# A graph network on one core: clears in the key phase, DVE's order in two projections, an output phase without loops, and aggregation's end sums on two queues

## What is computed

```python
h = jnp.maximum(_layernorm(x, axis=-1), 0.0)
x = x + _L0_gnn_ref(h, edge_index, ...)      # three attention convolutions, one head, sigmoid
h = jnp.maximum(_layernorm(x, axis=-1), 0.0)
x = x + _L1_gnn_ref(h, deg_isqrt[:, None], src, dst, edge_type_100, ...)   # relational, 4 bases
h = jnp.maximum(_layernorm(x, axis=-1), 0.0)
x = x + _L2_gnn_ref(h, edge_index, ...)      # attention, 8 heads
h = jnp.maximum(_layernorm(x, axis=-1), 0.0)
x = x + _L3_gnn_ref(h, edge_index, ...)      # messages from both ends of an edge, mean, linear
```

## Time and profile before

| | |
|---|---|
| three runs | 3926.29, 3939.06, 3943.65 us, median 3939.06 |
| profiled execution | 3923.35 us, its span 3921.4 us |
| busy share of the span | PE 58%, DVE 58%, POOL 55%, ACT 41% |
| mean granted TensorE clock | 0.79 |
| DMA, mean | 97 GB/s |

### The profile page before, as it was taken

How to read it: one execution, slowest core, us unless ns; L and a number is a source line. 1 busy time by engine, 2 the same in 40 slices (tenths; PEclk the granted TensorE clock), 3 DMA queues, 4 the chain that set the end, 5 groups by cost and what they waited for, 6 DMA issues and landing times. The chain is left out here.

```text
span 3921.4 us, 53964 instructions
## 1 busy us (share of the span) xinstructions
PE 2263.7 (58%) x12833; PEld 1777.4 (45%) x12833; DVE 2282.0 (58%) x8009; ACT 1610.7 (41%) x3565; POOL 2157.8 (55%) x2121
## 2 busy tenths in 40 slices
PE   1035899999898565465565567754526443344333
PEld 1023676676677554364464444434425332233222
DVE  4154999999898785334345378866575333333233
ACT  0005999999997573223323322324411222122100
POOL 3618765575564332581185255546500588888755
PEclk9998999999999786577577588887756666666665
DMA  2140122332231454651663733333304333333253
GB/s 64 27 181 20 44 90 87 100 103 87 87 92 39 133 157 116 161 139 42 186 174 87 203 95 99 87 98 81 90 16 118 109 74 64 75 74 65 51 145 117
DMA packets 569029, 380.48 MB, mean 97 GB/s; under 512 B 51389, under 2 KB 511942, under 8 KB 568386
## 3 DMA queue, kind: packets, MB, share of 16 engines
q1 hardware_dynamic: 510050, 329.99, 28.7%
q0 software_dynamic: 56000, 46.29, 6.4%
q10 hardware_dynamic: 2720, 1.23, 0.2%
HBM read 249.08 MB, written 153.32 MB: 103 GB/s over the span
## 5 line engine op out<-in xcount | busy, mean ns | idle before, releaser
L1309 POOL DMA_INDIRECT p_a<-t_d,k_map_ix x300 | 309.1, 1030 | 291.3 <-DMA p_a<-t_d 241.1
L807 POOL TENSOR_TENSOR a_rs<-a_ve,w_neg_half 128x16 f32<-128x16 f32 x113 | 330.1, 2922 | 241.7 <-DVE a_ve L743 227.7
L833 ACT ACTIVATE a_nr<-a_xb,a_nm,a_rs 128x128 f32<-128x128 f32 x882 | 369.9, 487 | 26.1 <-POOL a_nm L809 26.1
L2064 POOL DMA_INDIRECT e_a<-t_d,e_ix x200 | 210.4, 1052 | 277.1 <-DMA e_a<-t_s 219.2
L895 PE MATMUL a_ps<-w_ident,a_nr 128*128 128x128 f32 x1568 | 245.6, 280 | 128.8 <-DVE a_xb L754 47.3
L903 PE MATMUL a_ps<-a_ht,w_aug 128*128 128x512 f32 x588 | 312.7, 616 | 2.4 <-DVE a_ht L710 2.4
L895 PEld LDWEIGHTS a_ps<-w_ident,a_nr 128*128 128x128 f32 x1568 | 179.9, 143 | 277.0 <-issue 244.5
L1431 PE MATMUL p_pm<-w_aug,p_ht 128*128 128x130 f32 (+1 forms) x1600 | 277.1, 343 | 7.6 <-ACT p_ht L1392 3.8
L710 DVE TENSOR_TENSOR a_ht<-a_ps,a_ht 128x512 f32<-128x512 f32 x294 | 201.5, 686 | 134.7 <-ACT a_ps L848 111.0
L1431 PEld LDWEIGHTS p_pm<-w_aug,p_ht 128*128 128x128 f32 x1600 | 261.4, 250 | 21.4 <-ACT p_ht L1392 11.9
L1789 PE MATMUL c_pq<-layer_src,c_sel 128*128 (+1 forms) x800 | 194.3, 420 | 124.7 <-ACT c_sel L1760 72.2
(11 more groups left out here) (358 smaller groups left out, 6449.0 us busy)
## 6 DMA issues: line engine op xcount, KB each, us to landing
t_s<-p_a SPq DMA_DIRECT2D x100, 256.0 KB
c_a<-t_d SPq DMA_DIRECT2D x100, 256.0 KB
t_d<-c_a SPq DMA_DIRECT2D x100, 256.0 KB
a_xa<-in_x SPq DMA_DIRECT2D x98, 256.0 KB
out<-a_xb SPq DMA_DIRECT2D x98, 256.0 KB, 2.0
p_a<-t_s SPq DMA_DIRECT2D x75, 256.0 KB
p_a<-t_d SPq DMA_DIRECT2D x75, 256.0 KB
t_acc<-q_zt SPq DMA_DIRECT2D x3, 2171.5 KB
```

The lines of the kernel that those rows point to most:

```text
L807: nc.gpsimd.tensor_tensor(RS[:, z, :], VE[:, z, :], w["neg_half"][:, None, 0:J].to_broadcast([P, LNS, J]), ALU.pow).then_inc(s_rstd.sem, 1)
L833: last = nc.scalar.activation(NR[k][:, T.at(NORM[k], 2), cols(j)], normed_rows(T, k)[:, cols(j)], ACT.Identity, bias=NM[:, T.at(1, SHORT), ...
L1309: eng.indirect_dma_start(out=A[:, g, SRC, j, :], out_offset=None, in_=t[f"d{r}"], in_offset=bass.IndirectOffsetOnAxis(ap=k["map_ix"][:, b ...
L2064: eng.indirect_dma_start(out=A[:, g, side, j, :], out_offset=None, in_=t[f"d{r}"], in_offset=bass.IndirectOffsetOnAxis(ap=IX[:, g, what, j ...
```

## The change

- `keys`: behind each of the 100 scatters POOL clears a tile `idle` of 128x256, waiting for the clear before.
- `project`: in rounds 0 and 4 DVE's step n is now residual and hold first, statistics after. In round 0: residual(n-4), hold(n-3), turn(n). In round 4 the residual follows its hold by no step: hold(n-3), residual(n-3), turn(n). Rounds 1 and 2 keep their order.
- `aggregate`: SP issues four of the eight end-sum transfers, ahead of its loads and behind the last bank copy; ACT issues the other four. The two source-row transfers go ahead of ACT's last bank copy, with a semaphore of their own. ACT's sigmoid stands two blocks behind the widening, not one.
- `edge_outputs`: unrolled, a ring of 8 instead of 5, indices read in place instead of copied, a clear behind each scatter; TensorE and DVE take turn(n) and sum of block n ahead of product and end of block n-1.

```diff
@@ -219,6 +219,7 @@
         TMQ = sb("tmq", [P, T])
         DUMPC = sb("dumpc", [P, 1], I32)
         M1 = sb("m1", [P, T], I32)
+        IDLE, s_idle = sb("idle", [P, 256]), sem("idle")
         OF = sb("of", [T, 2, P])
         ENDROW = sb("endrow", [T, 2, T])
         OTHER = sb("other", [T, 2, T])
@@ -302,6 +303,9 @@
             for c in range(T):
                 eng.indirect_dma_start(out=t["maps"], out_offset=bass.IndirectOffsetOnAxis(ap=M1[:, c:c + 1], axis=0),
                                        in_=ID[:, c:c + 1], in_offset=None, bounds_check=NODES * WORDS - 1, oob_is_err=False).then_inc(s_map1, 16)
+                if c:
+                    eng.wait_ge(s_idle, c)
+                nc.gpsimd.memset(IDLE[:, :], 0.0).then_inc(s_idle, 1)
             eng.wait_ge(s_map1, 16 * T)
 
         @block.tensor
@@ -1358,16 +1362,19 @@
                 there(eng, b, SRC)
                 v.tensor_tensor(A[:, g, SRC, :, :], A[:, g, SRC, :, :], grow, ALU.add).then_inc(s_next, 1)
 
-            holds, residuals = (3, 4) if norm else (0, 1)
+            holds = 3 if norm else 0
+            residuals = holds if normed else holds + 1
             for n in range(BLOCKS + residuals):
+                if not normed and 0 <= n - residuals:
+                    residual(n - residuals)
+                if 0 <= n - holds < BLOCKS:
+                    hold(n - holds)
+                if normed and 0 <= n - residuals:
+                    residual(n - residuals)
                 if norm and n <= BLOCKS:
                     if n < BLOCKS:
                         there(eng, n)
                     mo.turn(eng, lambda m: A[:, n % RING, m // J, m % J, :], n, BLOCKS - 1)
-                if 0 <= n - residuals:
-                    residual(n - residuals)
-                if 0 <= n - holds < BLOCKS:
-                    hold(n - holds)
 
         @block.scalar
         def _(eng):
@@ -1634,6 +1641,14 @@
         ON_ACT = 13 if H == 1 else 0
         in_bank = lambda n: range(n * J, min(n * J + J, BLOCKS))
 
+        s_rows_in = sem("rows_in")
+
+        def end_sums(eng, tiles):
+
+            for j in tiles:
+                for s in range(2):
+                    eng.dma_start(ENDT[j:T:J, s, :], PART[2 * j + s:2 * j + s + 1, 0:BLOCKS, :]).then_inc(s_endt, 16)
+
         @block.sync
         def _(eng):
             def load(b, g):
@@ -1662,6 +1677,8 @@
                 carry_waits(eng, w)
                 eng.dma_start(block_rows(t[f"d{r + 1}"], b), A[:, g, :, :]).then_inc(s_out[g], 16)
 
+            eng.wait_ge(s_part, BANKS)
+            end_sums(eng, range(J // 2))
             stream(eng, (load, 0), *([(store_sel, 2)] if first else []), (store, 3))
             for g in range(GE):
                 eng.wait_ge(s_out[g], 16 * ROUNDS_E)
@@ -1709,7 +1726,7 @@
             for b in range(ON_ACT, BLOCKS):
                 v.tensor_tensor(heads_of(rows("dst", b)), heads_of(rows("dst", b)), over(tiles_of(ws, b)[:, :, 0:H]), ALU.mult).then_inc(s_own, 1)
             eng.wait_ge(s_new_pe, 1)
-            eng.wait_ge(s_endt, 16 * (2 * J + 2))
+            eng.wait_ge(s_rows_in, 32)
             v.tensor_tensor(NEW[:, :, :], PN[0:T, :, :], ENDT[:, 2:4, :], ALU.add).then_inc(s_new, 1)
             if ON_ACT:
                 eng.wait_ge(s_own_act, ON_ACT)
@@ -1738,15 +1755,14 @@
                             m = b * J + j
                             last = nc.scalar.activation(keep["dst"][:, m, 0:C], keep["dst"][:, m, 0:C], ACT.Copy, scale=ws[:, m, 0:1])
                         last.then_inc(s_own_act, 1)
+                if n == BANKS - 1:
+                    eng.wait_ge(s_ms, BLOCKS)
+                    for s, row in enumerate((0, P - 1)):
+                        eng.dma_start(ENDT[:, 2 + s:3 + s, :], keep["src"][row:row + 1, :, 0:C]).then_inc(s_rows_in, 16)
                 eng.wait_ge(s_part_pe, n + 1)
                 nc.scalar.activation(PART[:, n * J:n * J + len(in_bank(n)), :], PQ[n][0:2 * J, 0:len(in_bank(n)), :], ACT.Copy).then_inc(s_part, 1)
             eng.wait_ge(s_part, BANKS)
-            for j in range(J):
-                for s in range(2):
-                    eng.dma_start(ENDT[j:T:J, s, :], PART[2 * j + s:2 * j + s + 1, 0:BLOCKS, :]).then_inc(s_endt, 16)
-            eng.wait_ge(s_ms, BLOCKS)
-            for n, row in enumerate((0, P - 1)):
-                eng.dma_start(ENDT[:, 2 + n:3 + n, :], keep["src"][row:row + 1, :, 0:C]).then_inc(s_endt, 16)
+            end_sums(eng, range(J // 2, J))
             eng.wait_ge(s_new, 1)
             for n, row in enumerate((0, P - 1)):
                 eng.dma_start(keep["src"][row:row + 1, :, 0:C], NEW[:, n:n + 1, :]).then_inc(s_fix, 16)
@@ -1763,7 +1779,7 @@
                 wait(eng, s_u, b + 1)
                 nc.scalar.activation(PS[g][:, :, :], PS[g][:, :, :], ACT.Sigmoid).then_inc(s_sig, 1)
 
-            stream(eng, (widen, 0), *([(squash, 1)] if sigmoid else []))
+            stream(eng, (widen, 0), *([(squash, 2)] if sigmoid else []))
 
         @block.tensor
         def _(eng):
@@ -1775,7 +1791,7 @@
                         last = nc.tensor.matmul(PQ[n][0:2 * J, b - n * J, :], k["end_of"][:, m, :], keep["src"][:, m, 0:C],
                                                 start=j == 0, stop=j == J - 1)
                 last.then_inc(s_part_pe, 1)
-            eng.wait_ge(s_endt, 16 * (2 * J + 2))
+            eng.wait_ge(s_endt, 16 * 2 * J)
             for n in range(2):
                 for s in range(2):
                     last = nc.tensor.matmul(PN[0:T, n, :], k["cross"][:, 2 * n + s, :], ENDT[:, s, :], start=s == 0, stop=s == 1)
@@ edge_outputs
+    RING, BANKS = 8, 2
...
-        IX = sb("ix", [P, GE, J], I32)
-        ACC = sb("acc", [P, GE, J, M])
...
+        ACC = sb("acc", [P, RING, J, M])
...
+        IDLE = sb("idle", [P, 256])
...
         @block.gpsimd
         def _(eng):
...
+            for b in range(BLOCKS):
+                g = b % RING
+                eng.wait_ge(s_out_in, b + 1)
                 for j in range(J):
+                    m = b * J + j
-                    eng.indirect_dma_start(out=out, out_offset=bass.IndirectOffsetOnAxis(ap=IX[:, g, j:j + 1], axis=0),
+                    eng.indirect_dma_start(out=out, out_offset=bass.IndirectOffsetOnAxis(ap=k["out_s_ix"][:, m:m + 1], axis=0),
...
+                    if m:
+                        eng.wait_ge(s_idle, m)
+                    nc.gpsimd.memset(IDLE[:, :], 0.0).then_inc(s_idle, 1)
...
         @block.vector
...
-            stream(eng, (count_, 0), (finish, 1), (summed, 0))
+            for n in range(BLOCKS + 1):
+                if n < BLOCKS:
+                    summed(n)
+                if n:
+                    finish(n - 1)
...
         @block.tensor
...
-            stream(eng, (turn, 0), (product, 0))
+            for n in range(BLOCKS + 1):
+                if n < BLOCKS:
+                    turn(n)
+                if n:
+                    product(n - 1)
```

More of the change, by code:

```diff
@@ L2251, in edge_outputs @@
+        s_cnt, s_tp, s_s, s_mm, s_up, s_out_in, s_idle = (sem(n) for n in "cnt tp s mm up out_in idle".split())
+        s_load, s_out = ([sem(f"{n}{g}") for g in range(RING)] for n in ("load", "out"))
         block = ctx.enter_context(nc.Block())
-        before = lambda b, g: b - (1 if g == 0 else 2)
+        uses = lambda b: b // RING + 1
         @block.sync
         def _(eng):
-            def load(b, g):
-                wait(eng, s_out[g], (b // GE) * (16 * J))
-                carry_waits(eng, w)
+            for b in range(BLOCKS):
+                g = b % RING
+                if b >= RING:
+                    eng.wait_ge(s_out[g], (uses(b) - 1) * (16 * J))
```

75 lines of the change are left out of this document (35 added, 40 removed).

## The result

The changed kernel took 4086.39 us (median of four runs, 4079.69 to 4090.51) and the kernel before, beside it, 3940.16: a ratio of 1.038 (95% interval 1.035 to 1.041), 146 us slower. Its profiled execution took 4085.83 us, +162.5 against that of before, with a mean granted clock of 0.78.

A forecast was written before the change was run, and what follows sets the result against it. No engine bounds the kernel: each stage's longest loop sets its length, and stages add up. Terms -61 + 132 + 97 - 12 + 5 - 4 = +157 gave 4080 us profiled, 4096 us as median; range 4020 to 4145 us.

The forecast's parts named there:

- DVE order, round 0: `project`, round 0: hold ahead of statistics makes the path serial, 11.2 us a block against 5.46, +132 us (+95 to +144).
- if ACT's copy could pass apply: `project`: a condition under which the second rival had the earlier residual only free the ring; ACT's code order spoke against it.
- the second rival: `project`: the new order pays, round 0 unchanged and round 4 -53 us, giving 3814 us, faster; chance 0.07.
- Round 4: `project`, round 4: the serial path, now with the residual in it, replaces 8.30 us a block, +97 us (+51 to +106).
- I take 12.5: `project`, round 4: us a block assumed, between 10.5 with the fast product and 12.7 with the slow one.
- Key phase: `keys`: clears between scatters let TensorE's signals through, next stage loads at 210 instead of 271.08, -61 us (-66 to -50).
- 3 us for last landings and the barrier: Key phase: time allowed from the end of POOL's last scatter, at 207, to the next stage's load at 210.
- its weak bound of -50: Key phase: the gain if the table's zeroing and the scatters disturb each other, -50 us.
- Aggregate: `aggregate`, four rounds: split end sums and earlier row transfers -12 us (-16 to 0), later sigmoid +5 (0 to +8).
- the loads stay covered: `aggregate`: SP's loads, queued behind the end sums, are needed only over 10 us after the last bank copy.
- edge_outputs: `edge_outputs`: without loops, with a ring of 8 and clears, POOL alone sets the pace, 149 us, -4 us (-8 to +3).
- the third rival: Key phase: clears do not free TensorE's signal, waits stay and POOL takes 20 us longer, 4200 us; chance 0.07.
- the fourth: `project`: the reordering moves nothing that a wait rests on, 3867 us; chance 0.02.

The follow-up runs named there:

- e1_stats_first: The changed kernel with DVE's order of the kernel before in `project` (statistics, then residual, then hold): 3877.13 us, ratio 1.007 to the kernel before.
- e2_act_copies_first: The changed kernel, but ACT takes the copy of block n-1 and the sigmoid of n-2 ahead of apply(n) in rounds 0 and 4: 4075.45 us.
- e3_act_pe_first: As e2_act_copies_first, and TensorE also takes product(n-1) ahead of turn(n) in rounds 0 and 4: 3813.06 us, ratio 0.990.
- e6_before_clears: The kernel before with clears behind the key phase's scatters and nothing else of the change: 3889.67 us, ratio 0.986.
- e7_lag_one: The kernel of e3_act_pe_first with the sigmoid one block behind the widening again: 3824.25 us, ratio 0.969.
- e4_residual_early: The changed kernel with statistics first again in rounds 0 and 4, round 4's residual following its hold: 3830.60 us, ratio 0.995.

## Why the prediction was right, and where not

The sum was +157 us, the profiles show +162.5, the medians +146. The mechanisms came as written. That the touched stages add up to +156 is in part luck: the terms were off by 4, 13, 9, 5 and 2 us, in both directions.

**DVE order, round 0: +132 predicted, +128 found.** The steps are in the rows: shift to the destination's hold 7.66 us (7.26 read), hold to the next shift 3.67 (3.66 read), distances of 11.1 on average in the steady part (11.2 taken). That both holds wait for TensorE (though DVE waits longer for ACT's squashed rows ahead of them), that ACT and TensorE stand idle behind the shift, and that the clock falls came as written. `e1_stats_first` shows that all of it is DVE's order. One sentence was short of the truth: "if ACT's copy could pass apply" is not the point on which the second rival turns, as `e2_act_copies_first` shows; TensorE's product has to pass its transposes too. `e3_act_pe_first` also moved the squash ahead of apply, with the copy.

**Round 4: +97 predicted, +84 found.** The step that failed is "I take 12.5". One distance was 12.5, but it alternates with 11.4, the product taking 3.81 or 2.71 us: 23 x (12.5 - 11.95) is the 13 us. I had taken the slow end for most blocks, when the two ends, 10.5 and 12.7, stood in the text. (The upper bound does not follow from the text either: 12.7 us a block gives 23 x 4.4 = +101, not +106.)
The Trainium skill (TensorE: Matmul & The Clock Gate, section "HAM oscillation — how this bites in real kernels") says that a TensorE which waits between bursts starts each at half clock. The trace agrees: the transposes that open the blocks at 2852.3 and 2864.8 have a granted clock of 0.50. The step from there to whole blocks at the slow end, +106 here and +144 in round 0, was the prediction's own, and the measured terms are 22 and 16 us below it. Within most bursts the clock went back to 1.00: the product of 3.81 us had a mean granted clock of 0.54 and the next, of 2.71 us, 0.78, where the one of 4.05 us in the kernel before had 0.50.

**Key phase: -61 predicted, -52 found.** That the clears let TensorE's signals through was right, and POOL's end came at 209 instead of 207. (With free landings the stated sum gives 207 - 271 = -64, not -66.) The step that failed is "3 us for last landings and the barrier": it was 10.4, of which 8.2 are POOL's DRAIN. The term landed near its weak bound of -50, but not for the reason given there: zeroing and scatters do not disturb each other. The Trainium skill's rule (SBUF — State Buffer, section "SBUF: two separate sides"), by which only VectorE and GpSimd hold each other up and TensorE waits on nobody, speaks of access to SBUF. Read as if it covered signals too, it gave a loss of 20 us here; `e6_before_clears` shows a gain of 53.8.

**Aggregate: -12 and +5 predicted, -1.8 together found.** On the averages over fourteen profiles given above it is -11.4 for the end sums and +6.7 for the later sigmoid, -4.7 together: both terms were near, and the pair of profiles shows less because the kernel before was at its fastest in rounds 1 and 4. But -11.4 hides two errors. The cross product came 5 us earlier, not 3.3: with two queues the last transfer is issued 3.3 us after the bank copy as taken, but TensorE goes on 1.6 us behind it and not 3.1, as the two row transfers are no longer among those that it waits for. And "the loads stay covered" was too bold: they are covered, but the corrected rows now land 0.3 to 2.9 us later on average beside them. The later sigmoid costs 6.5 us in round 0 (5 taken, `e7_lag_one`) and nothing clear elsewhere.

**edge_outputs: -4 predicted, -2.4 found**, at POOL's pace of 1.50 us a scatter: 99.7 + 34.5 + 16.2 = 150.4. The old stage took 161.9 to 167.7 us in four profiles, the new one 160.7 to 162.5 in ten.

That the third rival (no signals freed) and the fourth (nothing moved) failed is shown by `e6_before_clears` and `e1_stats_first`. The second was right about what an earlier residual is worth: it gave 53 us for round 4, and `e3_act_pe_first` and `e4_residual_early` gained 50 and 45 against 232.4.

## What to carry over

In a software pipeline over in-order queues, write down for each wait which older block stands behind which newer one on every engine of the chain: moving a consumer ahead is free only where copies and products of its block can pass as well; otherwise a path that had two blocks' time gets one. When an edit bundles a harmful and a useful half, cost and try them apart. And where an engine becomes the last one in a stage, count its own drain at the barrier: it was there before, under other work.

## What the runs showed of the hardware

- POOL's DRAIN at a stage's end took 8.22 us behind 100 scatters, 4.13 behind 50 indirect transfers, 9.3 to 10.2 behind 99 or 100 gathers and 7.48 behind 400 mixed. It took 1.23 in a stage with no indirect transfer, where POOL's last instruction was still running, and 0.03 where POOL had done nothing. Behind `local_chain`'s 300 indirect transfers it took 9.2 us though the last of them had ended 143 us before, with other work of POOL in between. It is on the path wherever POOL ends last.
- While POOL issues scatters 1.28 us apart, TensorE's signal to DVE comes up to 19 us late; from 124.5 to 143 us of the kernel before DVE and TensorE execute nothing and the DMA share is 0.04. A clear of 0.33 us between scatters removes the delay, one of 0.15 us leaves 4 to 12 us of it, a met wait does not touch it. The last late signal, of a product that ends at 191.21, comes at 197.72, 10.6 us behind the end of the last scatter and 1.1 behind that of POOL's DRAIN.
- The kernel before has a second level, 3848 us on chip 8 against 3930 to 3951 on four other occasions, that the versions with clears do not show: `e1_stats_first` has, on chip 8, the same stages as the changed kernel and the kernel before have elsewhere. Round 4's project varies too: the same code took 232, 237, 238, 245 and 245 us.
